# Second attention by one head's 1024 keys per period, and turned maxima that join the query rows by an identity product

## The reference

```
xp = jnp.pad(x, ((0, 0), (p, p), (p, p), (0, 0)), mode='reflect')
q = _to_heads(_conv1x1(x, Wq, bq), N_HEADS)
k = _to_heads(_conv1x1(xp, Wk, bk), N_HEADS)
v = _to_heads(_conv1x1(xp, Wv, bv), N_HEADS)
energy = jnp.einsum('bhdq,bhdk->bhqk', q, k)
attn = jax.nn.softmax(energy, axis=-1)
out = jnp.einsum('bhdk,bhqk->bhdq', v, attn)
return gamma * out + x
```

## Time and profile before

| | us |
|---|---|
| median of 3 runs | 531.19 |
| the runs | 531.84, 525.45, 531.19 |
| the profiled execution's own time | 524.6 |
| its span, first to last instruction | 522.8 |
| mean granted TensorE clock | 0.987 |
| TensorE, VectorE, ScalarE, POOL busy | 493.7, 383.4, 348.8, 116.6 |

### The profile page before, as it was taken

One profiled execution on the slowest core, in us unless ns is written; L12 is line 12 of the kernel. 1 busy time (PEld: TensorE's weight loads), 2 busy tenths in 40 slices (PEclk: granted clock), 3 DMA queues, 4 the chain that ended last, 5 costly groups with the idle time before them and its releaser, 6 DMA issues.

```text
span 522.8 us, 10651 instructions
## 1 busy us (share of the span) xinstructions
PE 493.7 (94%) x4142; PEld 274.3 (52%) x4142; DVE 383.4 (73%) x739; ACT 348.8 (67%) x671; POOL 116.6 (22%) x110
## 2 busy tenths in 40 slices
PE   5899999999998999999999999999979999799997
PEld 2676676665443343343333334335565486655785
DVE  2566766557767899969799999988437646948996
ACT  2788888988444678768688887784747535437452
POOL 4010000122599797040203000014190000000000
PEclk9999999999999799999999999999999999989999
DMA  8900000000003400024250000004000000000011
GB/s 285 408 7 2 1 3 1 2 2 3 0 0 54 69 1 2 1 40 84 35 87 2 1 2 2 1 1 181 31 4 0 2 1 1 0 0 2 1 41 40
DMA packets 5522, 18.31 MB, mean 35 GB/s; under 512 B 1632, under 2 KB 1760, under 8 KB 5088
## 3 DMA queue, kind: packets, MB, share of 16 engines
q1 hardware_dynamic: 5472, 17.63, 11.9%
HBM read 11.86 MB, written 1.05 MB: 25 GB/s over the span
## 4 chain that ended last, share of the span: by engine, by line
PE 79%; DVE 7%; ACT 6%; POOL 4%; issue 3%; DMA 1%; SPq 0%; ACTq 0%; POOLq 0%; DVEq 0%
PE ps L471 70%; PE ps L631 7%; PE ps L821 2%; POOL stk3r L1843 1%; DVE mx L1488 1%; POOL stkr L1843 1%; ACT r_p L1147 1%; ACT r_p L1149 1%; POOL r_o L1823 1%; DVE r_p L1699 1%; DVE hidlo L1782 1%; ACT r_p L1333 1%; DMA xt<-in_xT 1%; DVE r_prt L1703 1%; ACT r_p L1183 1%
## 5 line engine op out<-in xcount | busy, mean ns | idle before, releaser
L1488 DVE TENSOR_REDUCE mx<-ps 128x2 f32<-128x1024 f32 x128 | 155.1, 1222 | 18.0 <-PE ps L471 16.8
L1333 ACT ACTIVATE r_p<-ps 128x512 f32<-128x512 f32 x256 | 140.1, 598 | 40.3 <-PE ps L471 37.3
L471 PE MATMUL ps<-r_p,r_v 128*32 128x256 f32 (+3 forms) x1344 | 95.2, 369 | 0.7 <-ACT r_o L1337 0.4
L471 PE MATMUL ps<-stkr 50*128 50x512 f32 (+1 forms) x384 | 86.4, 461 | 2.4 <-DVE mx L1488 1.1
L1569 DVE CUSTOM_DVE_ANT_0 r_p<-ps,r_tab 128x209 f32<-128x209 f32 (+1 forms) x128 | 45.0, 401 | 31.6 <-PE ps L471 31.6
L471 PEld LDWEIGHTS ps<-stkr 48*128 48x128 f32 (+1 forms) x384 | 35.7, 188 | 52.0 <-ACT r_p L1333 25.0
L1175 ACT ACTIVATE r_p<-r_p,mx 128x209 f32<-128x209 f32 (+1 forms) x128 | 57.5, 486 | 6.9 <-DVE mx L1569 6.5
L471 PEld LDWEIGHTS ps<-r_p,r_v 128*32 128x32 f32 (+3 forms) x1344 | 28.2, 109 | 50.2 <-ACT r_p L1333 23.4
L631 PEld LDWEIGHTS ps<-cst,r_p 128*95 128x95 f32 (+2 forms) x320 | 35.9, 148 | 17.7 <-issue 8.5
L631 PE MATMUL ps<-cst,r_p 128*95 128x128 f32 (+2 forms) x320 | 43.8, 276 | 1.5 <-ACT r_p L1183 1.0
L1183 ACT ACTIVATE r_p<-ps 95x512 f32<-95x512 f32 (+2 forms) x48 | 28.3, 589 | 9.0 <-PE ps L631 8.7
(11 more groups left out here) (211 smaller groups left out, 781.6 us busy)
## 6 DMA issues: line engine op xcount, KB each, us to landing
r_tab<-in_tab SPq DMA_DIRECT2D x4, 836.0 KB, 13.4
r_tab<-in_w SPq DMA_DIRECT2D x1, 2688.0 KB, 10.1
stkr<-nhi SPq DMA_DIRECT2D x32, 64.0 KB, 2.4
cst<-in_cst SPq DMA_DIRECT2D x1, 1252.5 KB, 18.3
r_tab<-in_tab SPq DMA_DIRECT2D x2, 532.0 KB, 7.2
r_tab<-in_tab SPq DMA_DIRECT2D x1, 1064.0 KB, 9.9
xt<-in_xT SPq DMA_DIRECT2D x4, 256.0 KB, 6.9
stkr<-nlo SPq DMA_DIRECT2D x16, 64.0 KB, 2.4
```

What stands on the lines that cost most here:

```text
L471: return nc.tensor.matmul(out, lhsT, rhs, start=start, stop=stop, **kw)
L1333: nc.scalar.activation(pa2[:, u % 12, :], ps[:, l2_bank(u), :], ACT.Exp).then_inc(sem("exp2"), 1)
L1488: v.tensor_reduce(mx[:, o:o + 2], ps[:, bank:bank + 2, :], AXIS.X, ALU.max).then_inc(sem("p1" if i % 8 < 7 else "p8"), 1)
```

## The change

- `l2_first`: a period's F covers one head and all 1024 keys. Both products lie in the same half of the rows; the head is e = 1 - r % 2.
- `l2_second`: the two S of a period belong to one head (e = u // 2 % 2) and two key chunks; two periods make the same four products as before in another order. S and F of a period are of different heads.
- `l2_values` runs in every second period, twice. Its wait is for the four Exp of its two periods. ScalarE's wait for a free place in `pa2` follows.
- VectorE reduces 1024 columns into one negated maximum in `mx`; `maxima` has two small instructions on `mx` instead of three on PSUM.
- `l2_turn` starts with a product of a rounded identity (`identr`, 128 rows) with the query rows, and adds the turned maxima to it with four rounded products. ScalarE copies the sum into the query stack (semaphore `joined`), between its two Exp of a period. VectorE's join is gone.
- `take2` comes behind the second Exp of its period.
- POOL makes `identr` by one copy after it has cleared `zmax`.

The number of S banks and the wait of S(u) for the Exp of S(u-3) are as before.

```diff
@@ PE: slot_free
-                if kind == "first" and i % 8 == 7:
-                    pe.wait_ge(sem("zmax"), i // 8 + 1)
-                elif kind in ("first", "max"):
+                if kind == "max":
+                    pe.wait_ge(sem("joined"), i + 1)
+                elif kind == "first":
                     pe.wait_ge(sem("p1"), freed[e])
@@ PE: l2_first
-                qt, kh = r // 2 % 4, r % 2
+                qt, e = r // 2 % 4, 1 - r % 2
...
-                for e in (1, 0):
-                    rows = slice(64 * e, 64 * e + PARTS)
-                    last = mm(ps[:, bank + e, :], stack(b)[rows, 0, pr, q0:q0 + 128], stack(b)[rows, 1, pr, tile(kh)])
+                rows = slice(64 * e, 64 * e + PARTS)
+                for kh in range(2):
+                    if r == 0 and kh:
+                        pe.wait_ge(sem("sp2"), 3)
+                    last = mm(ps[:, bank + kh, :], stack(b)[rows, 0, pr, q0:q0 + 128], stack(b)[rows, 1, pr, tile(kh)])
@@ PE: l2_turn
+                b, pr, qh = phase(m)
+                if m == 0:
+                    pe.wait_ge(sem("zero_max"), 2)
+                mm(ps[:, bank, :], identr[:, :], stack(b)[:, 0, pr, tile(qh)], stop=False)
                 pe.wait_ge(sem("zmax"), m + 1)
                 for qt in range(4):
                     o = TILE * (m % 2) + C * qt
-                    last = nc.tensor.transpose(ps[:, bank, C * qt:C * (qt + 1)], zmax[:, o:o + C], ident)
+                    last = mm(ps[:, bank, C * qt:C * (qt + 1)], zmaxr[:, o:o + C], identr[:, :], start=False, stop=qt == 3)
@@ PE: l2_second
-                m, c, e = u // 16, u // 2 % 8, u % 2
+                m, c, e = u // 16, 2 * (u // 4 % 4) + u % 2, u // 2 % 2
                 b, pr, qh = phase(m)
                 if u % 16 == 0:
-                    pe.wait_ge(sem("p1"), freed[at["max", m, 0]])
+                    pe.wait_ge(sem("joined"), m + 1)
@@ PE: l2_values
-                pe.wait_ge(sem("exp2"), 2 * j + 2)
+                pe.wait_ge(sem("exp2"), 4 * (j // 2) + 4)
...
-                                  pa2[:, (2 * j + e) % 12, 256 * half:256 * half + 256], start=c == 0, stop=c == NCH - 1)
+                                  pa2[:, (4 * (j // 2) + 2 * e + j % 2) % 12, 256 * half:256 * half + 256], start=c == 0, stop=c == NCH - 1)
@@ PE: the loop
-                if p >= 2:
+                if p > 2 and p % 2:
+                    l2_values(p - 3)
                     l2_values(p - 2)
@@ ACT: l2_entry
+                if kind == "max":
+                    b, pr, qh = phase(i)
+                    act.wait_ge(sem("s1_2"), taken[e])
+                    nc.scalar.activation(stack(b)[:, 0, pr, tile(qh)], ps[:, bank, :], ACT.Copy).then_inc(sem("joined"), 1)
@@ ACT: weights2
-                    act.wait_ge(sem("pv2"), (u - 12) // 2 + 1)
+                    act.wait_ge(sem("pv2"), 2 * ((u - 12) // 4) + 2)
@@ ACT: the loop
-                if p >= 8 and p % 8 == 2:
-                    take2(p // 8 - 1)
                 if p >= 0:
                     weights2(2 * p)
...
                 if p >= 0:
                     weights2(2 * p + 1)
+                if p >= 8 and p % 8 == 2:
+                    take2(p // 8 - 1)
@@ DVE: maxima
-                v.tensor_reduce(w, mx[:, 16 * (m % 2):16 * (m % 2) + 16].rearrange("p (k g) -> p g k", k=2), AXIS.X, ALU.max).then_inc(sem("m16"), 1)
...
-                v.tensor_scalar(zr[:, :, PARTS], w, -1.0, None, ALU.mult).then_inc(sem("zhi"), 1)
+                v.tensor_copy(zr[:, :, PARTS], w).then_inc(sem("zhi"), 1)
...
-                v.scalar_tensor_tensor(zr[:, :, PARTS + 1], w, -1.0, z[:, :, PARTS], ALU.mult, ALU.subtract).then_inc(sem("zmax"), 1)
+                v.tensor_tensor(zr[:, :, PARTS + 1], w, z[:, :, PARTS], ALU.subtract).then_inc(sem("zmax"), 1)
@@ DVE: l2_entry
-                    v.tensor_reduce(mx[:, o:o + 2], ps[:, bank:bank + 2, :], AXIS.X, ALU.max).then_inc(sem("p1" if i % 8 < 7 else "p8"), 1)
+                    v.tensor_reduce(mx[:, o:o + 1], ps[:, bank:bank + 2, :].rearrange("p b n -> p (b n)"), AXIS.X, ALU.max, negate=True).then_inc(sem("p1"), 1)
...
-                elif kind == "max":
-                    b, pr, qh = phase(i)
-                    dve.wait_ge(sem("s1_2"), taken[e])
-                    v.tensor_tensor(stack(b)[:, 0, pr, tile(qh)], ps[:, bank, :], stack(b)[:, 0, pr, tile(qh)].bitcast(F32), ALU.add).then_inc(sem("p1"), 1)
@@ POOL
+            pool.wait_ge(sem("zero_max"), 1)
+            g.tensor_copy(identr[:, :], ident).then_inc(sem("zero_max"), 1)
```

More of the change, by code:

```diff
@@ L212, in l2_order @@
         p += kind in ("first", "max")
-        f += kind == "max" or kind == "first" and i % 8 < 7
+        f += kind == "first"
         slot.append(-1 if loose else slot[at[kind, i, 0]] if k else c)
@@ L279, in build @@
         zmax = zmaxr[:, :].bitcast(F32)
+        identr = rounded("identr", "r_tab", W3N + 3072, [C, C])
         r_stk = sb("r_stk", [C, 12288])
@@ L805, in l2_first @@
                 b, pr, qh = phase(r // 8)
-                qt, kh = r // 2 % 4, r % 2
+                qt, e = r // 2 % 4, 1 - r % 2
                 if b and r % 32 == 0:
                     pe.wait_ge(sem(f"stk2_{b}"), 24 * 16)
-                elif r in (0, 1, 8, 16):
-                    pe.wait_ge(sem("sp2"), {0: 2, 1: 3, 8: 4, 16: 8}[r])
+                elif r in (0, 8, 16):
+                    pe.wait_ge(sem("sp2"), {0: 2, 8: 4, 16: 8}[r])
                 q0 = qh * TILE + 128 * qt
-                for e in (1, 0):
-                    rows = slice(64 * e, 64 * e + PARTS)
-                    last = mm(ps[:, bank + e, :], stack(b)[rows, 0, pr, q0:q0 + 128], stack(b)[rows, 1, pr, tile(kh)])
+                rows = slice(64 * e, 64 * e + PARTS)
[3 more added lines that the diff above has]
+                    last = mm(ps[:, bank + kh, :], stack(b)[rows, 0, pr, q0:q0 + 128], stack(b)[rows, 1, pr, tile(kh)])
                 last.then_inc(sem("s1_2"), 1)
             def l2_turn(m, bank):
+                b, pr, qh = phase(m)
+                if m == 0:
+                    pe.wait_ge(sem("zero_max"), 2)
+                mm(ps[:, bank, :], identr[:, :], stack(b)[:, 0, pr, tile(qh)], stop=False)
                 pe.wait_ge(sem("zmax"), m + 1)
@@ L1301, in l2_entry @@
                 bank = 2 * (slot[e] % 2)
-                if kind == "proj" and k:
+                if kind == "max":
+                    b, pr, qh = phase(i)
+                    act.wait_ge(sem("s1_2"), taken[e])
+                    nc.scalar.activation(stack(b)[:, 0, pr, tile(qh)], ps[:, bank, :], ACT.Copy).then_inc(sem("joined"), 1)
+                elif kind == "proj" and k:
                     low2(i)
@@ L1340, in _ @@
                 p = q - AHEAD
-                if p >= 8 and p % 8 == 2:
-                    take2(p // 8 - 1)
                 if p >= 0:
                     weights2(2 * p)
-                if q <= PERIODS:
+                if q <= PERIODS + 2:
                     for e in range(ends[q - 2] if q > 1 else 0, ends[q - 1]):
@@ L1456, in _, with maxima @@
             v = nc.vector
-            def maxima(m, bank):
-                w = ps[:, bank, 0:8]
+            def maxima(m):
+                w = mx[:, 8 * (m % 2):8 * (m % 2) + 8]
                 half = slice(TILE * (m % 2), TILE * (m % 2 + 1))
@@ L1462, in maxima @@
                 dve.wait_ge(sem("p1"), freed[at["first", 8 * m + 7, 0]])
-                dve.wait_ge(sem("p8"), m + 1)
-                v.tensor_reduce(w, mx[:, 16 * (m % 2):16 * (m % 2) + 16].rearrange("p (k g) -> p g k", k=2), AXIS.X, ALU.max).then_inc(sem("m16"), 1)
-                dve.wait_ge(sem("m16"), m + 1)
                 if m > 1:
@@ L1486, in l2_entry @@
                     dve.wait_ge(sem("s1_2"), taken[e])
-                    o = 16 * (i // 8 % 2) + 8 * (i % 2) + i // 2 % 4 * 2
-                    v.tensor_reduce(mx[:, o:o + 2], ps[:, bank:bank + 2, :], AXIS.X, ALU.max).then_inc(sem("p1" if i % 8 < 7 else "p8"), 1)
+                    o = 8 * (i // 8 % 2) + 2 * (i // 2 % 4) + 1 - i % 2
+                    v.tensor_reduce(mx[:, o:o + 1], ps[:, bank:bank + 2, :].rearrange("p b n -> p (b n)"), AXIS.X, ALU.max, negate=True).then_inc(sem("p1"), 1)
                     if i % 8 == 7:
-                        maxima(i // 8, bank)
-                elif kind == "max":
-                    b, pr, qh = phase(i)
-                    dve.wait_ge(sem("s1_2"), taken[e])
-                    v.tensor_tensor(stack(b)[:, 0, pr, tile(qh)], ps[:, bank, :], stack(b)[:, 0, pr, tile(qh)].bitcast(F32), ALU.add).then_inc(sem("p1"), 1)
+                        maxima(i // 8)
                 elif kind == "split":
@@ L1841, in blank @@
                     for rows in (slice(32, 64), slice(96, 128)):
-                        pool.wait_ge(sem("blank"), blanks[0]) if blanks[0] else pool.wait_ge(sem("zero_max"), 1)
+                        pool.wait_ge(sem("blank"), blanks[0]) if blanks[0] else pool.wait_ge(sem("zero_max"), 2)
```

## The result

The changed kernel took 544.98 us (median of 4 runs, 542.05 to 558.13), the kernel before 528.32 (median of 4, 521.10 to 531.84). The ratio is 1.040, interval 1.022 to 1.057: slower. The forecast was 546.

A forecast was written before the change was run, and what follows sets the result against it. TensorE was taken to bind plain periods, the changed cycle to wait on an Exp through three score banks. 7.5 + 8.4 + 1.3 + 1.6 = +18.8 us on 524.6 gave 543.4; with run spread 546 was predicted, range 528 to 562.

The forecast's parts named there:

- The plain cycle: Full part: fourth score product waits for the first's Exp, so two periods take 2.61 us against 2.48; +7.5 us over 58.
- Join cycle: Phase end: the maxima product waits for ScalarE's copy of the turned sum, making that cycle 0.73 us longer.
- Copy: Phase end: the accumulator's copy behind both Exp lets the values start at 1.96 instead of 1.61 us, 0.35 later.
- Turn: Phase end: identity product 0.24 plus four rounded products 0.59, 0.83 us in all, against 0.59 for the old transposes.
- The 4.9 us beside the old turn: Phase end: if the old turn were full-precision and the rounded one a quarter of it, the sum would be 4.9 less.
- F is no longer held by VectorE's reduce: Phase end: old waits of the maxima product, 0.27 and 0.44 us, go; maxima lie in SBUF and the reduce finishes earlier.
- 7.5 + 8.4: Full part: 58 longer two-period cycles add 7.5 us, 14 phase ends at 0.60 each add 8.4.
- Ahead of the full part: Before score products start, maxima products share a half of the rows and run one behind the other: +1.3 us.
- Behind it: After the full part, periods without maxima products and the last two values products: together +1.6 us.
- the pairing wins: Rival, full part: fourth score product unhindered, cycles of 2.43 or 2.15 us; faster, 517 or 504 us; chance 0.10.
- Cheap phase ends: Rival, phase ends: turn at its lower bound, join and copy waits half hidden; no difference, 531 to 538; chance 0.22.
- The clock rival: Rival, TensorE's granted clock: new pauses cause two to four further falls; slower still, 552 to 565 us; chance 0.12.

The follow-up runs named there:

- the F product issued twice: Changed kernel with the second maxima product of the second maxima pair issued twice in three of four two-period cycles a phase: 550.70 us, ratio 1.048 to the kernel before.
- one V a period: Changed kernel with one values product issued every period instead of two every second period: 535.38 us, ratio 1.020 to the kernel before.
- S3 behind the values: Changed kernel with the fourth score product of each two-period cycle issued behind the two values products instead of ahead: 593.69 us, ratio 1.113 to the kernel before.
- one V a period and the join first: Changed kernel with one values product every period and ScalarE's copy of the turned sum ahead of its period's first Exp: 541.87 us, ratio 1.012 to the kernel before.
- second profile: Profile of the unaltered changed kernel taken beside the experiments: span 544.3 us, granted clock 0.975.
- the grouping alone: Changed kernel with the old turn (four full-precision transposes) and the old join (VectorE's add) put back: 532.32 us, ratio 1.016 to the kernel before.
- the turn and join on the kernel before: Kernel before with only the identity product, rounded turn products and ScalarE's copy of the sum added: 529.07 us, ratio 1.012 to the kernel before.
- the second set of runs: Changed kernel run again unaltered beside the experiments: 551.15 us (546.09 to 553.36), ratio 1.050 to the kernel before.
- the two versions with the join on VectorE: Changed kernel with VectorE copying the turned sum, 533.83 us; changed kernel with old transposes and VectorE's add, 532.32 us.

## Why the prediction was right

**The plain cycle.** Forecast 2.61, measured 2.60, by the chain that was named: S0 to S3 1.18 and 1.18, S3 to V 0.43 and 0.42, V V 1.00 and 1.00 (300.15 to 301.15). It is shown from three sides: more TensorE work in the idle time costs nothing (the F product issued twice), the same work with a V inside the burst is faster (one V a period), and another S put in the fourth place waits the same 1.19 (S3 behind the values).

**The phase's end.** Join cycle: +0.73 forecast, +0.73 measured (3.33 against 2.60), and 0.65 or 0.73 come back when the join moves to a better place. Copy: 0.35 and 0.36; 0.33 comes back. Turn: 0.83 and 0.82, but the split was wrong: the identity product takes 0.34 from its start to the next and the four rounded products 0.48, where I had 0.24 and 0.59; that the two errors cancel is luck. (The 4.9 us beside the old turn are the lower bound again, 14 x 0.35; a quarter of the old turn's 0.59 would have given 6.2.) F is no longer held by VectorE's reduce: true in the changed kernel, where F stands right beside S0 at 307.53.

**The sum.** In the full part, up to the first S without F, the kernel before takes 172.18 us (172.48 to 344.66) and the changed one 190.36 (175.35 to 365.71): +18.2, where 7.5 + 8.4 = 15.9 was forecast.

It is not a sum of 14 equal phases, as I had it. From one small maxima instruction to the next, the eight phases without other work and at full clock in both kernels are 1.08 to 1.10 longer, as forecast (1.14), and one is 0.89 longer. Two with a projection are only 0.32 and 0.34 longer (14.15 and 14.47, 14.14 and 14.48): the projection's products stand between the pairs of a burst (229.05 to 230.97), and S3 then goes out without a wait (second two pairs at 230.97, values 0.66 behind them). In the other three the clock fell in one or both kernels, and they are 0.49, 4.28 and 3.42 longer. At full clock throughout, the full part would be some 13 to 14 us longer (an estimate: 1.09 for two of the three, 0.3 to 1.8 for the third, which has a projection too). So taking all 14 phases as clean was some 2 us too much, and falls of the clock more than filled that.

Ahead of the full part I had +1.3: here the first S comes 2.9 us later (175.35), with the clock at 0.50 at 170 to 172; with one V a period and the join first, at full clock there, it comes 1.9 later (174.41). That term was mis-sized by 0.6; that more of the twelve periods are TensorE's than the nine I counted is likely, and not shown. Behind it I had +1.6; the last V V ends 16.6 us after 365.71, against 14.7 in the kernel before, +1.9. The three make 22.9, and the span grew by 21.5: what lies behind the values took 1.4 less in this execution (162.0 against 163.5 us), for a reason that stays open.

All told 542.05 and 542.36 us at a mean clock of 0.987, the clock of the execution with 524.6: +17.6 against the +18.8 of the sum. VectorE's work fell by 8.7 us (9.8 in the second profile) and not by 14, which changes nothing in the sum, as VectorE isn't the bound.

**The rivals.** That the pairing wins is refuted: no cycle was near 2.15, and the grouping alone is at 1.016 (1.010 to 1.022). Cheap phase ends are refuted for the changed kernel; with the turn and join on the kernel before the waits do overlap. The clock rival happened in part: one run of the first four took 558.13 us at 0.92, and in the second set of runs the changed kernel had 0.960 to 0.975 and 546 to 553 us. The prediction read one fall in the trace of the kernel before, and there are two: the second, at about 455 to 462 us, lies behind the stage. The second profile of the changed kernel has five, three more, and that execution took 546.09 us, where the rival had 552 to 565 for two to four more: a fall was priced too high. The forecast's 546 holds with the clock of the first set and lies 5 us low with that of the second. That it meets the 544.98 to within a microsecond is partly luck: it was taken from the spread of three runs. What sets the clock stays open.

**Where my later reasoning failed.** The repair of moving S3. I wrote the new wait of the one product that I moved and not those of the other three, and it came out about 42 us slower than the changed kernel (593.69 against 551.15) instead of 10 faster.

No version beat the kernel before. One V a period with the join first has the shorter phase, 10.88 against 11.23, and loses it again, in part at both ends of the stage and in part to the clock.

## What to carry to other kernels

Before grouping work of one kind to save switches, count the buffers between producer and consumer: a burst longer than the ring waits for the consumer's latency once each time round, and what stands behind the burst is added to that. An instruction moved to a less busy engine has to be judged by what stands ahead of it in that queue and who waits for the buffer that it frees. When a buffer is passed on in a ring, write down the waits of every member after a move, not of the moved one alone.

## What the runs showed of the hardware

The granted clock in forty equal slices of the span, in the kernel before and in the second profile of the changed one:

```profile
PEclk9999999999999799999999999999999999989999
PEclk9999999999998889989999999999999999879999
```

In the kernel before it fell to 0.50, 1.2 of 2.4 GHz, twice, near 176 and near 456 us, for about 7 us each; in the changed one five times, for some 27 us in all. With one V a period and the join first it stayed there for 20 us at once:

```profile
176.00:178.00 2.00, 2.00 (x9) 1.19 (x9) 2.00 (x3) 2.00 (x5) 2.00 (x1) 1.00 0.14 25
186.00:188.00 2.00, 2.00 (x16) 0.70 (x12) 1.06 (x2) 0.92 (x3) 1.92 (x3) 0.50 0.00 0
196.00:198.00 2.00, 2.00 (x14) 0.70 (x12) 1.41 (x2) 1.09 (x2) 2.00 (x2) 0.50 0.00 0
200.00:202.00 2.00, 2.00 (x19) 1.17 (x17) 1.23 (x1) 1.30 (x3) 1.92 (x3) 1.00 0.00 0
```

TensorE is recorded busy in all of 186 to 198 us and the clock does not come back. The Trainium skill ("TensorE: Matmul & The Clock Gate", "A second HAM failure mode: psum-queue depth-cycling") ties such swings to short idles between groups of products; the traces agree in that the changed kernel, which has more waits, had more falls (mean clock 0.977 to 0.997 in the kernel before, 0.960 to 0.987 in all but one run of the changed one), but two pauses ahead of a fall could be filled and it still came, and the two versions with the join on VectorE, whose cycles have the same pause ahead of S3, stayed at 0.981 to 0.990. Executions of one and the same kernel differ by 16 us (the changed one, 542.05 at 0.987 to 558.13 at 0.920) and by up to 33 us (S3 behind the values, 582.53 at 0.935 to 615.52 at 0.864), so that the phase length, not the total, told the versions apart. In the one of 558.13 us the granted clock was 0.95 from 10 us on wherever it hadn't fallen, and never 1.00.

From start to start a rounded 128x128 product behind another takes 0.12 us (four in 0.48, 307.05 to 307.53), a transpose of the same size 0.15, a full-precision product 0.26.
